# Recurrent branch plus six local-attention layers: variance spread over the partitions by one matmul, its root on 256 columns, weight and table loads at other half steps

## The reference

```python
def ffn_layer(x, g, bln, W1, b1, W2, b2):
    mu = x.mean(-1, keepdims=True)
    var = ((x - mu) ** 2).mean(-1, keepdims=True)
    xn = (x - mu) / jnp.sqrt(var + 1e-05) * g + bln
    hg = xn @ W1 + b1
    a, gate = jnp.split(hg, 2, -1)
    return a * jax.nn.gelu(gate, approximate=False) @ W2 + b2
```

## Time and profile before

| | us |
|---|---|
| median of 3 runs | 1691.66 |
| lowest and highest of them | 1690.63, 1693.77 |
| the profiled execution, its own time | 1692.23 |
| its span in the profile | 1690.4 |
| busy in the span: PE, PEld | 1604.2, 1372.8 |
| DVE, ACT, POOL | 1367.0, 1350.4, 1327.8 |
| mean granted TensorE clock | 0.992 of full speed |

### The profile page before, as it was taken

The page is one execution under the profiler, slowest core; times in us unless marked ns, Lnnn a source line. Parts: engine busy times, 40 slices in busy tenths (PEclk is TensorE's granted clock), DMA queues, the critical chain, the costliest instruction groups (busy, mean ns, idle before and its releaser), DMA issues. The chain is left out here.

```text
span 1690.4 us, 50127 instructions
## 1 busy us (share of the span) xinstructions
PE 1604.2 (95%) x19920; PEld 1372.8 (81%) x19920; DVE 1367.0 (81%) x2005; ACT 1350.4 (80%) x2517; POOL 1327.8 (79%) x1276
## 2 busy tenths in 40 slices
PE   4799999999999999999999999999999999999985
PEld 2578888888888888888888888888888888788773
DVE  5788888888888888888888888888888877888733
ACT  3477888888888888888888888888888888888874
POOL 8888889888889888889888889788888777667720
PEclk9999999999999999999999999999999999999997
DMA  3433323434333334233344232343342332222220
GB/s 111 118 112 104 105 75 89 118 90 121 90 88 92 96 112 122 78 100 92 87 120 118 76 105 79 94 126 101 88 109 69 84 87 75 71 67 65 67 83 28
DMA packets 184947, 156.91 MB, mean 93 GB/s; under 512 B 111502, under 2 KB 156172, under 8 KB 184716
## 3 DMA queue, kind: packets, MB, share of 16 engines
q1 hardware_dynamic: 184716, 153.70, 32.3%
HBM read 27.30 MB, written 1.05 MB: 17 GB/s over the span
## 5 line engine op out<-in xcount | busy, mean ns | idle before, releaser
L1487 POOL TENSOR_TENSOR qk<-qk,t 128x1024 f32<-128x1024 f32 x192 | 456.5, 2379 | 100.1 <-DVE qk L1260 100.0
L1257 DVE TENSOR_TENSOR t<-ps_qn,tab 128x512 f32<-128x512 f32 x384 | 264.5, 689 | 136.0 <-ACT sq L1015 125.2
L1499 POOL TENSOR_TENSOR qkr<-qk,rinv 128x1024 f32<-128x1024 f32 x192 | 361.9, 1906 | 7.7 <-PE ps_tr L750 0.4
L737 PE MATMUL ps_qn<-w_hi,xs_hi 128*128 128x512 f32 x576 | 259.4, 450 | 25.5 <-POOL xs_lo L1535 11.7
L1002 ACT ACTIVATE pbd<-ps_tr 64x512 f32<-64x512 f32 x384 | 226.1, 589 | 64.7 <-PE ps_tr L750 61.6
L1015 ACT ACTIVATE sq<-ps_qn 128x512 f32<-128x512 f32 x384 | 229.0, 597 | 50.6 <-PE ps_qn L739 45.9
L1260 DVE TENSOR_TENSOR qk<-ps_qn,tab 128x512 f32<-128x512 f32 x384 | 261.2, 680 | 0.0
L1051 ACT ACTIVATE qbd<-ps_tr 64x512 f32<-64x512 f32 x384 | 227.1, 592 | 33.1 <-PE ps_tr L763 27.9
L738 PE MATMUL ps_qn<-w_lo,xs_hi 128*128 128x512 f32 x576 | 228.9, 397 | 0.0
L739 PE MATMUL ps_qn<-w_hi,xs_lo 128*128 128x512 f32 x576 | 228.3, 396 | 0.0
L1270 DVE TENSOR_REDUCE ss<-sq 128x32 f32<-128x2048 f32 x96 | 216.6, 2256 | 0.0
(11 more groups left out here) (153 smaller groups left out, 3224.4 us busy)
## 6 DMA issues: line engine op xcount, KB each, us to landing
v_own<-v_new SPq DMA_DIRECT2D x96, 512.0 KB, 3.2
v_back<-v_new SPq DMA_DIRECT2D x96, 384.0 KB, 3.5
v_back<-v_own SPq DMA_DIRECT2D x96, 128.0 KB, 2.3
kT<-kT SPq DMA_DIRECT2D x84, 128.0 KB, 2.6
w_raw<-in_Wqkv SPq DMA_DIRECT2D x18, 512.0 KB, 5.1
rot<-in_rot SPq DMA_DIRECT2D x48, 128.0 KB, 2.6
xsh<-x SPq DMA_DIRECT2D x192, 32.0 KB, 2.4
fx<-xmid SPq DMA_DIRECT2D x96, 64.0 KB, 2.1
```

Source lines behind the costliest of these rows:

```text
L737: mm(ps_qn[bank][:, :], xs_hi[b][:, :], w_hi[:, part], start=True, stop=False)
L1257: v.tensor_tensor(t2[:, part].rearrange("p (h s d) -> p h s d", s=2, d=DH // 2), swapped, tab[:, 2 * k + 1:2 * k + 2, :].rearrange("p o (s ...
L1487: g.tensor_tensor(qk[b][:, part], qk[b][:, part], t2[:, part], ALU.add).then_inc(added[b], 1)
L1499: g.tensor_tensor(qkr[b][:, part].rearrange("p (h d) -> p h d", d=DH), qk[b][:, part].rearrange("p (h d) -> p h d", d=DH), rinv[b][:, k * ...
```

## The change

The variance is computed by one matmul with a 128 x 128 matrix of 1/128 (`mean_w`) over all 256 columns of `fsq`, so that it stands on every partition at once (`ffn_variance`, PE, half 0, between `out_projection` and the recurrent `rec_output`). It takes a place of its own, `variance`, in ring `qn`. The two narrow matmuls, the 2 extra columns of the Q/K norm, `spread_roots`, `ffn_broadcast`, and DVE's multiplication in `take_out1` go. In their place:

- ACT `ffn_log` (half 0, after `rec_output`, ahead of `evac_q`): a log into `fix` and a copy with eps into `var`, 256 columns each, from PSUM with a bias column.
- ACT `ffn_root` (half 1, after `inverse_root`, ahead of `evac_probs`): an exp into `fsq` and its square into `fix`.
- POOL `scale_variance` (half 1, where `spread_roots` was): `fix` times `var`. ACT `ffn_root_fix` (half 1, after the last gelu): 1.5 - 0.5 `fix`.
- POOL `scale_centred` (half 1, after `floor`): `fxn` = `fsq` times `fc`. POOL `fix_normalised` (half 0 of the next step, after the first `add`): `fxn` times `fix`.
- `round_fxn` waits for that and takes the gain g as a scale column as well as the bias column.

Loads: `ln_gb` moves from (3, 0) to (3, 1) and waits for `fxn_high`; b1 gets a semaphore of its own and moves to (4, 0); W2 and b2 move to (4, 1); Wo moves from the end of (1, 1) to the start of (2, 0); the rotary table of step i+1 is loaded at step i without a wait for that step's own table (before: that of step i+2, after such a wait).

```diff
@@ qn_order
-        order += rec_fills(i, b, HIDDEN_AT, "hidden") + rec_fills(i, b, OUT_AT, "branch")
+        order += rec_fills(i, b, HIDDEN_AT, "hidden") + ["variance"] * (b == 0 and valid(i - 3)) + rec_fills(i, b, OUT_AT, "branch")
@@ SP load_weights, load_out_weights, load_rotary
-                    if (i.t, b) == (1, 1):
-                        wait_fill(sp, pv_full, pv_order, i, ("out", 1))
-                        w.load_wo(sp, l)
-                    elif (i.t, b) == (3, 0):
-                        sp.wait_ge(fxn_ready, TILES * l)
+                    if (i.t, b) == (3, 1):
+                        sp.wait_ge(fxn_high, 2 * TILES * l)
                         w.load_gb(sp, l)
-                    elif (i.t, b) == (3, 1):
                         sp.wait_ge(w.w1_ready, l)
                         w.load_w1(sp, l)
-                        wait_fill(sp, qn_done, qn_order, i, ("up", 2))
+                    elif (i.t, b) == (4, 0):
+                        wait_fill(sp, qn_done, qn_order, i - 1, ("up", 2))
                         w.load_b1(sp, l)
-                    elif (i.t, b) == (4, 0):
+                    elif (i.t, b) == (4, 1):
...
+                def load_out_weights(i):
+                    if i.t != 2 or not i.past_first_layer:
+                        return
+                    wait_fill(sp, pv_full, pv_order, i - 1, ("out", 1))
+                    w.load_wo(sp, i.layer)
...
-                    if not valid(i + 2):
-                        return
-                    sp.wait_ge(tab_ready, i.n + 1)
-                    w.load_rot(sp, (i + 2).tile)
+                    if not valid(i + 1):
+                        return
+                    after_first(sp, tab_ready, i.n, i)
+                    w.load_rot(sp, (i + 1).tile)
@@ PE
-                    if b == 0 and valid(n):
-                        wait_fill(pe, qn_done, qn_order, i, "centre")
-                        for s in range(B):
-                            last = mm(ps_pv[bank][:, VAR + s:VAR + s + 1], fsq[:, s, :], mean_col[:, :], start=True, stop=True)
...
-                    mm(ps_pv[bank][:, DOWN], ones[:, :], flat(diag), start=True, stop=True).then_inc(pv_full[bank], 1)
+                    wait_fill(pe, qn_done, qn_order, i, "centre")
+                    bank = next_bank(i, "variance")
+                    mm(ps_qn[bank][:, 0:B * P], mean_w[:, :], flat(fsq), start=True, stop=True).then_inc(qn_full[bank], 1)
@@ ACT
+                def ffn_log(i):
...
+                    after_first(act, fxn_raw, n.n, n)
+                    mean_sq = ps_qn[bank][:, 0:B * P]
+                    f(flat(fix), mean_sq, ACT.Ln, bias=eps_col[:, :]).then_inc(var_log, 1)
+                    f(flat(var), mean_sq, ACT.Identity, bias=eps_col[:, :]).then_inc(qn_done[bank], 1)
+
+                def ffn_root(i):
...
+                    act.wait_ge(var_log, n.n + 1)
+                    f(flat(fsq), flat(fix), ACT.Exp, scale=-0.5).then_inc(var_root, 1)
+                    act.wait_ge(var_root, n.n + 1)
+                    f(flat(fix), flat(fsq), ACT.Square).then_inc(var_sq, 1)
+
+                def ffn_root_fix(i):
...
+                    act.wait_ge(var_t, n.n + 1)
+                    f(flat(fix), flat(fix), ACT.Copy, bias=1.5, scale=-0.5).then_inc(var_fix, 1)
@@ ACT round_fxn
-                    wait_fill(act, pv_done, pv_order, i - 1, ("out", 1))
+                    act.wait_ge(fxn_raw, m.n + 1)
...
-                        f(out[:, :, :], fxn[:, :, :], ACT.Identity, bias=ln_gb[:, SM_B:SM_B + 1], scale=1.0).then_inc(fxn_high, 1)
+                        f(out[:, :, :], fxn[:, :, :], ACT.Identity, bias=ln_gb[:, SM_B:SM_B + 1], scale=ln_gb[:, SM_G:SM_G + 1]).then_inc(fxn_high, 1)
@@ POOL
+                def scale_variance(i):
...
+                    pool.wait_ge(var_sq, n.n + 1)
+                    g.tensor_tensor(fix[:, :, :], fix[:, :, :], var[:, :, :], ALU.mult).then_inc(var_t, 1)
+
+                def scale_centred(i):
...
+                    after_first(pool, fxn_ready, n.n, n)
+                    g.tensor_tensor(fxn[:, :, :], fsq[:, :, :], fc[:, :, :], ALU.mult).then_inc(centre_scaled, 1)
+
+                def fix_normalised(i):
...
+                    pool.wait_ge(var_fix, m.n + 1)
+                    pool.wait_ge(centre_scaled, m.n + 1)
+                    g.tensor_tensor(fxn[:, :, :], fxn[:, :, :], fix[:, :, :], ALU.mult).then_inc(fxn_raw, 1)
@@ POOL half
                     if b == 1:
-                        spread_roots(i)
+                        scale_variance(i)
+                    else:
+                        fix_normalised(i)
```

More of the change, by code:

```diff
@@ L486, in layer_tiles, with layers @@
     return w
-def layers(nc, a, x, xmid, branch, ident, w, rec):
+def layers(nc, a, x, xmid, branch, ident, eps_col, w, rec):
     with ExitStack() as ctx:
@@ L583, in wait_fill, with after_first_fill @@
                 eng.wait_ge(sems[bank], n)
+        def after_first_fill(eng, sems, order, i, what, step):
+            if not step.first:
+                wait_fill(eng, sems, order, i, what)
         def ring_free(eng, done, bank, count):
```

167 lines of the change are left out of this document (78 added, 89 removed).

## The result

The changed kernel takes 1701.35 us (1698.99 to 1704.39), the kernel before 1691.66 us (1690.63 to 1693.77): a ratio of 1.0055, with a 95% interval of 1.0038 to 1.0072. The change makes the kernel slower by 0.55%. The forecast was 1690.0 us, with "within 0.2%" the likeliest outcome; 1701.35 is inside the range of 1677 to 1702, at its edge.

The account below looks back on a forecast made before the run. The prediction took PE's own work, start to start, as the bound. Its terms summed to +0.3 us, 2 us was taken off, and from the median that gave 1690 us, with a range of 1677 to 1702.

Parts of the forecast that it names:

- half 1, L855 gone: Half 1: 0.42 us of PE work goes, 0.2 or 0.1 is lost again; net -0.30 in 32 halves, -9.6 us.
- half 0, matmul and q: Half 0: matmul +0.07 us, `scores` stall 0.15 for q; +0.22 in 33 halves, +7.3 us.
- i.t = 4 to 6: Half 0 at i.t = 4, 5, 6: weight pieces on ACT and later rounding add 0.2 in 15 halves, +3 us.
- new layers: New layer, five times: POOL has no gap, ACT's rounding waits for it; +1.4 us each, +7 us.
- loads at i.t = 3: At i.t = 3: SP's wait no longer delays `move_v`, so four longer distances shrink; -5 us.
- start: Start of the run: DVE's 4.82 us wait for `move_v` goes, PE had some slack; -3 us.
- last 8 steps: Last 8 steps: `branch` stalls 0.7, next chunk 0.5; +0.5 in half 0, -0.3 in half 1; +1.6 us.
- drain: Drain: Newton steps leave POOL in step 50, -2.5; two other places with ACT longer, +1.5; sum -1 us.
- taken off: Whole sum: 2 us taken off because stall terms were thought more likely too large than too small.
- Rival C: Whole kernel: PE isn't bound by its own work, so removing some gives nothing; +9.6, 1700 us; chance 0.05.
- 25 equal steps: Of 36 distances between centring matmuls in steps 3 to 39, 25 are 31.69 to 31.72 us; evidence for PE as bound.

Follow-up runs that it names:

- run 6: The changed kernel with VectorE's subtraction for the low part of W1 put ahead of its two V copies: 1698.24 us, ratio 1.0028 to the kernel before.
- run 10: The changed kernel with VectorE's copy of the first V chunk in half 1 taking 256 of its 512 columns: 1699.79 us, ratio 1.0037 to the kernel before.
- run 3: The changed kernel with a filler matmul of 256 columns at the old place of L855: 1704.31 us, ratio 1.0071 to the kernel before.
- run 11: The changed kernel with both the first V chunk's copy and VectorE's sums of squares halved in half 1: 1691.11 us, ratio 0.9999 to the kernel before.
- run 12: The changed kernel with VectorE's sums of squares halved in half 1, the V copy whole: 1701.36 us, ratio 1.0042 to the kernel before.
- run 4: The changed kernel with ScalarE's logarithm of the variance moved from half 0 to the head of half 1: 1693.65 us, ratio 1.0012 to the kernel before.
- run 8: The changed kernel without the correction step (two ScalarE passes and two GpSimd products a step): 1693.19 us, ratio 1.0007 to the kernel before.
- run 1: The kernel before with the moved loads alone, the variance as before: 1682.59 us, ratio 0.9941 to the kernel before.
- run 9: The changed kernel with the logarithm in half 1, variance behind the branch, and the root behind the probabilities in a layer's first step: 1686.48 us, ratio 0.9959.

## Why the prediction was wrong

By its own terms, against what the profiled executions measured. (The measured terms of steps 3 to 40 are split over all 37 distances, with the new layers and i.t = 4 to 6 as what they have over a plain step.)

| term | forecast | measured |
|---|---|---|
| half 1, L855 gone | -9.6 | 37 x -0.10 = -3.7 |
| half 0, matmul and q | +7.3 | 37 x +0.13 = +4.8 |
| i.t = 4 to 6 | +3 | +3.4 |
| new layers | +7 | +5.2 |
| loads at i.t = 3 | -5 | -5.4 |
| start | -3 | -4.5 |
| last 8 steps | +1.6 | +5.9 |
| drain | -1 | +1.1 |
| taken off | -2 | 0 |
| sum | -1.7 | +6.8 (spans: +6.7) |

The table accounts for the two profiled executions. The medians are 9.7 us apart; of the 3 us between, the low clock in step 44 (run 6) is the one part that a trace suggests.

**The step that failed** is the first of the half-1 argument: from 741.00 - 740.23 = 0.77 in the earlier trace rows it took 0.42 us as L855's share of PE's time, on the ground that PE is the bound. It then asked what is late next, but began to look at `evac_probs`, a whole `scores` further on. What is late next stood one matmul further on: the last `up` part needs a bank that DVE had just freed, 0.06 us before PE took it. The term is 5.9 of the 8.5 us by which the sum was off the spans. It could have been seen in the trace of before. DVE's copy ends at 739.96 + 0.69 = 740.65 and L876 starts at 740.71, while L855 starts at 740.45. One small distance can be chance: in run 10, where that wait is gone, the same distance is 0.07 to 0.08 us. That it was 0.053 to 0.057 in 44 half steps of 44 was the sign that this matmul is bound by that signal, though no idle time is shown ahead of it, because something else filled the time. The premise, that PE at 199 of 200 us busy is bound by its own work, was what hid this. Runs 3 and 10 to 12 show it false for half 1.

Rival C said so and gave 1700 us, with a chance of 0.05. That its time came so close is in part luck: it gave up all 9.6 us of half 1, of which 3.7 came, and it had the last eight steps 4.3 us too cheap. I set 25 equal steps against it. Equal steps show only that the same chain of waits repeats, not that PE's work is that chain. The Trainium skill (Perfetto Trace Analysis, "Identifying the Most-Contended Engine"), which the forecast weighed and set aside, says to judge how near TensorE is to its limit by, among other things, the share of its weight loads, and not by matmul busy time. The trace agrees here: that share was 87% in the window, and work worth 0.43 us went in and out at a cost of 0.10.

**The last eight steps** were seen rightly in kind. The forecast has `branch` waiting 0.7 (measured 0.66) and the next chunk 0.5 (0.42). The two waits are 1.08 together. It counted only +0.5 for half 0, since DVE already held PE at `mask`. The row that it had for that is the 1.02 of step 44; the steps around it had only 0.63 to give back, and in half 1. By the measured halves it is +1.53 up to half 1 and -0.76 in half 1, of which 0.63 is the wait at the mask. That is +0.76 or +0.77 in a step where the forecast had +0.2. So half 0 was sized 1 us too small, and half 1 gave 0.5 us more than forecast. Step 44 (+2.5) is outside the bounds of any single step; run 6 names its parts, of which the meeting (1.6) was in no term.

**Half 0** was +0.13 and not +0.22. The mechanism holds, as run 4 shows: ACT's two instructions at 475 and 477 ns, q evacuated from 594.17, which is 3.59 behind the centring matmul, where 724.28 in the forecast is 3.66.

**The new layers** came out by the mechanism that was written down, POOL late, ACT's rounding waiting for it, +1.28 against +1.4; run 8 takes the load away and 1.14 of it goes.

**The loads** gave 5.4 at i.t = 3 against 5. The start gave 4.5 in this pair of executions; over the 12 kernels with the new loads, after among them, the first centring stands at 109.3 to 112.2 us, on the mean 110.6, and over the two with the old ones at 113.99 and 113.50. That is 3.1 us, what was forecast. In the medians the loads are worth 0.6% (run 1), 9 to 10 us, where the forecast had 8.

**The drain** was forecast as a gain and was a loss of 1.1. It has three stretches. From the centring of step 48 to that of 49 it is 31.77 us instead of 30.53 (+1.24): `scores` wait up to 2.9 us for q, where they waited 1.9. From 49 to 50 it is 19.97 instead of 18.17 (+1.80): PE waits 2.01 us for the probabilities, where it waited 1.11. From 50 to the end it is 1.96 us shorter: the wait of the earlier trace rows shrank as foreseen, from 3.25 to 1.12. Windows view of the middle stretch, before and below it after:

```profile
1637.76:1655.93 18.17, 13.26 (x143) 11.59 (x141) 4.26 (x10) 10.03 (x19) 4.14 (x8) 1.00 0.04 8
...
1644.60:1664.57 19.97, 14.19 (x140) 12.55 (x138) 4.28 (x9) 11.46 (x22) 4.73 (x5) 0.91 0.04 9
```

The granted clock was 0.91 there in after, that is at its lower level for 3.4 us. In runs 9 to 11, with the new way to the variance, the same wait of 1.96 to 2.01 us and the clock at 1.00 throughout, the stretch is 18.62 to 18.65. So of the 1.80 us some 1.3 came with the clock and 0.5 with the new work. Without the 1.3 the drain would be about level, where the forecast had -1.

**The 2 us taken off**, because "a late engine catches up in gaps that I counted as full", had no row behind it. Run 6 shows the other direction: an engine that comes late meets something that it would have missed.

## What to carry to other kernels

Where PE is always busy, ask of a matmul that you want to remove not how long it is, but which signal the instruction behind it needs and when that came. If it came while the matmul ran, the matmul is filler and its removal gives little, here 0.10 of 0.42 us.

A new tile in a two-bank ring changes the partner of every bank behind it. Write out the ring before and after and look for a slow reader in the new place ahead of a consumer that had a fast one; here swapping two entries took 7.1 us of 1697.1 by the timelines and 0.56% by the ratios.

Time a change's parts apart where they don't touch. Here +1.2% and -0.6% lay in one number, and the half worth keeping was the one that moved only loads.

## What the runs showed of the hardware

A `tensor_tensor_scan` of VectorE with 128 columns takes 0.46 us. When it came up behind two others 0.17 us after GpSimd had begun a product of 128 x 1024 from SBUF, it took 2.06 us (2.06 or 2.07 in all eight kernels in which this happened, 0.49 or less in the other six, where it began 0.2 us ahead of the product), and it ended about when the first of GpSimd's two products did (1464.25 + 1.95 to 2.01 = 1466.2 to 1466.3; the scan's row ends at 1466.48). Two instructions that read PSUM, the subtraction of the maximum (1.23 us) and the rotation (0.68 us), ran beside such products at the same length as in all other steps.

The Trainium skill (SBUF — State Buffer, "SBUF: two separate sides") states that VectorE, where it has two inputs in SBUF, and GpSimd share a port pair as an exclusive lock for a whole instruction. The trace agrees: 1.6 us of waiting for 0.46 us of work.

The granted TensorE clock fell to the lower of its two levels for 3.4 us at the end of a wait of 2.40 us, in seven of eight executions, and did not fall in step 44 where the wait was 1.12 us or less. For those 3.4 us PE's rows are longer, a 512-column matmul of a chunk 0.63 where it is 0.40 (L742, run 8), and the step was 1.1 to 1.3 us longer.

What ACT's and POOL's new instructions take for 256 fp32 columns, by form in the groups of after (line, instruction, count, busy us, mean ns, idle before):

```profile
L1105 ACT ACTIVATE fxn_hi<-fxn,ln_gb 128x256 fp32r<-128x256 f32 x48 | 29.6, 617 | 4.8 <-POOL fxn L1553 4.8
...
L1079 ACT ACTIVATE fix<-ps_qn,eps_col 128x256 f32<-128x256 f32 x48 | 22.8, 475 | 5.6 <-PE ps_qn L854 5.6
...
L1553 POOL TENSOR_TENSOR fxn<-fxn,fix 128x256 f32<-128x256 f32 x48 | 35.4, 737 | 17.2 <-ACT fix L1096 17.2
```

The rounding with a bias column and a scale column takes 617 ns. The same rounding with the bias column alone took 527 ns before the change: a second column costs 90 ns, in 96 instructions.
